# All last tokens formed at the start: a cross-attention kernel whose context is cut into 512-token parts of 528-column rows

## What is computed

```python
x = x + xattn(layernorm(x), ctx_1024, ...)   # 16 heads of 32, 1601 context tokens a batch, stablemax weights
x = x + attn(layernorm(x), ...)              # 8 heads of 64, causal, inside a batch
x = x + ffn(layernorm(x), ...)               # 2 shared experts and the top 2 of 8, hidden 2048
# stablemax: s = where(v >= 0, v + 1, 1 / (1 - v)); s / sum(s)
```

## Time and profile before

| | us |
|---|---|
| median of three runs | 1272.42 (1272.4 to 1272.51) |
| the profiled execution | 1272.52 |
| its span, first to last instruction | 1270.8 |
| TensorE matmuls, busy | 1260.8 |
| VectorE, busy | 649.4 |
| ScalarE, busy | 634.2 |
| GpSimd, busy | 437.4 |

### The profile page before, as it was taken

How to read it: one execution, slowest core, us unless ns; L and a number is a source line. 1 busy time by engine, 2 the same in 40 slices (tenths; PEclk the granted TensorE clock), 3 DMA queues, 4 the chain that set the end, 5 groups by cost and what they waited for, 6 DMA issues and landing times.

```text
span 1270.8 us, 29915 instructions
## 1 busy us (share of the span) xinstructions
PE 1260.8 (99%) x13126; PEld 1097.3 (86%) x13126; DVE 649.4 (51%) x936; ACT 634.2 (50%) x1085; POOL 437.4 (34%) x203
## 2 busy tenths in 40 slices
PE   9999999999999999999999999999999999999998
PEld 8888888888788888888789789798989999999997
DVE  5333453444463363463354454766776555565655
ACT  4445454464545544545444646646544443554443
POOL 1445345544555545545546535200032000100000
PEclk9999999999999999999999999999999999999999
DMA  6131011021011012012012111764556499999990
GB/s 244 50 103 51 18 56 50 23 68 67 19 64 68 18 56 101 19 64 68 18 51 105 51 56 43 284 255 157 179 195 224 148 348 365 340 344 347 357 396 35
DMA packets 32775, 174.89 MB, mean 138 GB/s; under 512 B 5944, under 2 KB 8152, under 8 KB 14464
## 3 DMA queue, kind: packets, MB, share of 16 engines
q1 hardware_dynamic: 30896, 168.16, 36.0%
q0 software_dynamic: 1744, 4.76, 1.2%
HBM read 166.84 MB, written 6.06 MB: 136 GB/s over the span
## 4 chain that ended last, share of the span: by engine, by line
PE 98%; DVE 1%; DMA 0%; ACT 0%; issue 0%; DVEq 0%; SPq 0%
PE bank L740 23%; PE bank L728 22%; PE bank L1079 11%; PE sc L1096 9%; PE sc L756 8%; PE sc L941 7%; PE bank L769 4%; PE sc L960 3%; PE bank L960 3%; PE bank L833 1%; PE bank L796 1%; PE bank L887 1%; PE bank L898 1%; PE sc L898 1%; DMA ctxt<-in_ctx 0%; PE sc L999 0%
## 5 line engine op out<-in xcount | busy, mean ns | idle before, releaser
L587 POOL TENSOR_TENSOR xn<-xn,tt 128x1024 f32<-128x1024 f32 x96 | 230.1, 2397 | 330.9 <-DVE tt L1325 329.7
L1208 ACT ACTIVATE tt<-sc 128x512 f32<-128x512 f32 (+1 forms) x208 | 107.8, 602 | 351.5 <-PE sc L756 351.4
L1423 DVE TENSOR_TENSOR wsl<-ring,wsh 128x2048 fp32r<-128x2048 f32 x72 | 166.8, 2316 | 111.0 <-ACT wsh L1163 107.9
L1312 DVE TENSOR_SCALAR kk<-bank,bkt 128x512 f32<-128x512 f32 (+2 forms) x130 | 80.8, 622 | 213.6 <-PE bank L728 213.2
L728 PE MATMUL bank<-cxh,wkh 128*128 128x512 f32 (+2 forms) x512 | 181.1, 354 | 1.5 <-DVE va L1320 1.0
L728 PE MATMUL bank<-cxl,wkh 128*128 128x512 f32 (+2 forms) x512 | 174.6, 341 | 0.0
L728 PE MATMUL bank<-cxh,wkl 128*128 128x512 f32 (+2 forms) x512 | 174.1, 340 | 0.0
L740 PE MATMUL bank<-wvh,cxh 128*128 128x512 f32 (+1 forms) x416 | 163.5, 393 | 0.0
L740 PE MATMUL bank<-wvl,cxh 128*128 128x512 f32 (+1 forms) x416 | 162.7, 391 | 0.0
L740 PE MATMUL bank<-wvh,cxl 128*128 128x512 f32 (+1 forms) x416 | 162.2, 390 | 0.0
L1163 ACT CAST wsh<-ring 128x2048 fp32r<-128x2048 f32 x72 | 137.4, 1909 | 48.0 <-PE sc L1096 20.9
(11 more groups left out here) (270 smaller groups left out, 2024.2 us busy)
## 6 DMA issues: line engine op xcount, KB each, us to landing
ring<-in_w SPq DMA_DIRECT2D x112, 1024.0 KB, 6.1
ctxt<-in_ctx SPq DMA_DIRECT2D x15, 1024.0 KB, 4.9
ctxt<-in_ctx SPq DMA_DIRECT2D x8, 642.0 KB, 3.9
ctxt<-in_ctx SPq DMA_DIRECT2D x10, 512.0 KB, 3.6
wqt<-in_wo SPq DMA_DIRECT2D x4, 1024.0 KB, 4.8
wqt<-in_aq SPq DMA_DIRECT2D x4, 1024.0 KB, 5.3
wqt<-in_ap_ SPq DMA_DIRECT2D x4, 1024.0 KB, 6.9
yrows<-K SPq DMA_DIRECT2D x1, 2048.0 KB, 9.1
```

The costliest lines, as they stand in the source:

```text
L587: e.tensor_tensor(dacc[0:kn, y, :], dacc[0:kn, y, :], tt[0:kn, w, :], ALU.add).then_inc(s["da_pool"], 1)
L1423: e.tensor_tensor(wsl[m % 3][:], ring[slot(unit_split(m))][:], wsh[m % 3][:].bitcast(F32), ALU.subtract).then_inc(s["wl_dve"], 1)
```

## The change

- The last 65 tokens of all eight batches are one extra load (`tails`), 520 columns in a row of 528. At the start all their keys are formed, as 48 matmuls of 260 columns each for batches 0 to 3 and 4 to 7 (`tail_keys`), and their values in five groups (`tail_values`): four of 128 tokens, each two batches' 64 tokens, and one of the eight very last tokens. Keys and values are stored to memory (`ktail`, `vtail`).
- In each batch SP loads the batch's tail keys back into `ktb` (`load_tail`, slot 1) and its tail values into their slot of `va` (`load_tail_values`, slot 11).
- The rest is 24 parts of 512 tokens; each has four key groups of 512 columns and four value groups. The key groups of a batch's first part move one slot back, to its slots 9 to 12 of the batch before. Slot 10 of a batch has no value group, slot 8 no key group.
- For chunks 99 to 102 the value group stands in the slot of its own number, before it was so for 101 to 103. Chunk 103, a tail, has none.
- The queries are three rounded products of 16 matmuls of 512 columns, with high and low parts of x (`xTh`, `xTl`) and of the weights.
- The start is put in a new order: tail keys, tail values between the turns of x, queries, the keys of part 0 (now 512 tokens), values 0 and 1. Loads of wk, tails, wv, x and wq come in halves.
- Rows of `cxh`, `cxl`, `ctxt` and `kk` have 528 columns, of which a part fills 512. Pads are put between buffers. GpSimd's descriptor scratch goes from its default to 4096 bytes.

```diff
-SPANS = ((0, 512), (512, 512), (1024, 256), (1280, 321))
-WID = 512
+WID = 528
+TAIL = 65
-NPART = len(PARTS)
+NPART = 3 * NB
...
 def key_groups(slot):
+    groups = []
     for i in range(1, NPART):
+        f = first(i - 1) + ((i - 1) % 3 == 2)
+        groups += [(i, slot - f)] * (0 <= slot - f < 4)
+    return groups
...
 def values_in(slot):
-    if slot + 2 < NCH - 3:
-        return slot + 2
-    return slot if NCH - 3 <= slot < NCH else None
+    if slot + 2 < NCH - 5:
+        return None if is_tail(slot + 2) else slot + 2
+    return slot if NCH - 5 <= slot < NCH - 1 else None
...
-    uses = [("k", 0, g) for g in range(4)] + [("v", 0), ("v", 1)]
+    uses = [("vt", j) for j in range(5)] + [("k", 0, g) for g in range(4)] + [("v", 0), ("v", 1)]
...
+        ktb = sb("ktb", [P, 2, 4, TAIL])
+        ceh, cel = sb("ceh", [P, 4, 8], F32R), sb("cel", [P, 4, 8], F32R)
+        sb("pad9", [P, 8])
...
+            for h in range(2):
+                c = slice(2 * h, 2 * h + 2)
+                e.dma_start(wkt[:, c, :], wk[:, c, :]).then_inc(wk_in[h], 16)
+                e.dma_start(tail_raw[:, c, :], tails[:, c, :]).then_inc(tails_in[h], 16)
...
+            def load_tail(b):
+                if b >= 2:
+                    e.wait_ge(s["s_pe"], PER * (b - 1))
+                e.dma_start(ktb[:, b % 2, :, :].rearrange("p g n -> p (g n)"),
+                            ktail[:, 4 * TAIL * b:4 * TAIL * (b + 1)]).then_inc(s["kt_in"], 16)
+            def load_tail_values(b):
+                n = PER * b + PER - 1
+                e.wait_ge(s["p_pe"], n - VR + 1)
+                e.dma_start(va[0:TAIL, n % VR, :], vtail[b]).then_inc(s["vt_in"], 16)
...
+            def tail_values(j):
+                dst, kn = take("vt", j), (8 if j == 4 else P)
+                if j < 2:
+                    e.wait_ge(s["kt_dve"], 8 + 2 * j + 2)
...
             def turn(t, dst):
                 e.wait_ge(s["xn_dve"], t + 1)
+                if t < 2:
+                    e.wait_ge(s["kt_dve"], 16)
+                else:
+                    e.wait_ge(s["xt_dve"], t - 1)
...
+            tail_values(0)
+            tail_values(1)
             for t in range(2):
                 turn(t, bank[2 + t])
+            tail_values(2)
             for t in range(2, 4):
                 turn(t, bank[t])
+            tail_values(3)
+            tail_values(4)
+            e.wait_ge(s["xt_dve"], 4)
             for g in range(4):
+                queries(g)
+            for g in range(4):
+                keys(0, g)
             for n in range(2):
                 values(n)
...
+            for g in range(4):
+                tail_keys(0, g)
+            for h in range(2):
+                e.wait_ge(x_in[h], 16)
                 for t in range(2 * h, 2 * h + 2):
                     stats_of(0, t)
                 for t in range(2 * h, 2 * h + 2):
                     rows(0, t)
+                for g in range(2 * h, 2 * h + 2):
+                    tail_keys(1, g)
...
-    nc = bacc.Bacc("TRN2", target_bir_lowering=False, num_devices=1)
+    nc = bacc.Bacc("TRN2", target_bir_lowering=False, num_devices=1, dynamic_dma_scratch_size=4096)
```

More of the change, by code:

```diff
@@ L45, in first, with is_tail, tokens, place @@
 def first(i):
[L47 to L63, removed]
+    return PER * (i // 3) + 4 * (i % 3)
+def is_tail(n):
+    return n % PER == PER - 1
+def tokens(n):
+    return TAIL if is_tail(n) else P
+def place(n):
+    b, j = divmod(n, PER)
+    return 3 * b + j // 4, j % 4
+def formed(n):
+    return (PER - 1) * (n // PER) + n % PER
 def key_groups(slot):
-    early, late = [], []
+    groups = []
     for i in range(1, NPART):
[L70 to L79, removed]
+        f = first(i - 1) + ((i - 1) % 3 == 2)
+        groups += [(i, slot - f)] * (0 <= slot - f < 4)
+    return groups
 def ending(slot, lag):
@@ L196, in build @@
         xn = sb("xn", [P, 4, D])
+        with ExitStack() as over:
+            xTh = over.enter_context(nc.sbuf_tensor("xTh", [P, 4, D], F32R))
         with ExitStack() as over:
@@ new lines, in tail_values @@
+            def tail_values(j):
+                dst, kn = take("vt", j), (8 if j == 4 else P)
+                col = 260 * (j // 2) + P * (j % 2)
+                if j < 2:
+                    e.wait_ge(s["kt_dve"], 8 + 2 * j + 2)
+                if j == 4:
+                    e.wait_ge(s["tl_dve"], 3)
+                for c in range(4):
+                    if j == 0 and c % 2 == 0:
+                        e.wait_ge(s["wvl_dve"], c // 2 + 1)
+                    for x_, (a, b) in enumerate(three):
+                        m = e.matmul(dst[0:kn, :], (ceh, cel)[a][:, c, :] if j == 4 else
+                                     (cxh, cxl)[a][:, 1, c, col:col + P], (wvh, wvl)[b][:, c, :],
+                                     start=(c == 0 and x_ == 0), stop=(c == 3 and x_ == 2))
+                m.then_inc(s["vt_pe"], 1)
@@ L744, in scores @@
             def scores(n):
-                i, k, kn = chunk(n)
-                u, b, c0 = i % 2, n // PER, 256 * (n - group_of(n)[0])
+                i, k = place(n)
+                b, c0, kn = n // PER, 256 * (n - group_of(n)[0]), tokens(n)
                 if n >= 2:
@@ L755, in scores @@
                         r = slice(32 * h, 32 * h + 32)
-                        m = e.matmul(sc[0:kn, h, c0 + 64 * g:c0 + 64 * g + 64], kk[r, u, g, k * P:k * P + kn],
-                                     qc[r, g, 64 * b:64 * b + 64], start=True, stop=True)
+                        key = ktb[r, b % 2, g, :] if is_tail(n) else kk[r, i % 2, g, k * P:k * P + P]
+                        m = e.matmul(sc[0:kn, h, c0 + 64 * g:c0 + 64 * g + 64], key, qc[r, g, 64 * b:64 * b + 64],
+                                     start=True, stop=True)
                 m.then_inc(s["s_pe"], 1)
             def weighted(n):
-                kn, b = chunk(n)[2], n // PER
+                kn, b = tokens(n), n // PER
                 head, tail = n % PER == 0, n % PER == PER - 1
-                e.wait_ge(s["proj_read"], use["v", n] + 1)
+                if tail:
+                    e.wait_ge(s["vt_in"], 16 * (b + 1))
+                else:
+                    e.wait_ge(s["proj_read"], use["v", n] + 1)
                 e.wait_ge(s["f_dve"], 2 * n + 2)
@@ L1032, in pe @@
                     denominators(b)
-                for i, g in early + late:
+                for i, g in key_groups(n):
                     keys(i, g)
@@ L1201, in act @@
                 for m in group(n):
-                    kn = chunk(m)[2]
+                    kn = tokens(m)
                     if m >= TR:
@@ L1502, in vector @@
             e.tensor_copy(kio[:], iotai[:, P:P + 120].rearrange("p (k e) -> p k e", e=8)).then_inc(s["iota_dve"], 1)
-            values(0)
-            values(1)
+            for g in range(4):
+                keys(0, g)
+            for n in range(2):
+                values(n)
             count = [0]
@@ L1651, in vector @@
                     weights(m, 1)
-                for i, g in late:
-                    keys(i, g)
                 for b, g, m in finished(n)[1]:
```

345 lines of the change are left out of this document (207 added, 138 removed).

## The result

The changed kernel takes 1277.72 us (median of 8 runs, 1274.45 to 1278.83), the kernel before 1272.41 us: a ratio of 1.0037, 95% interval 1.0027 to 1.0046. It is slower by 0.4%, where 1263.3 us and "faster" at 0.91 were forecast. Its times spread over 4.4 us, those of before over 0.3 us, and they lie in groups: 1274.5 (granted clock 0.998 over the run) and 1277 to 1279 us (0.995 to 0.996). The profiled execution is one of the first group: 1274.46 us, span 1272.7 us.

The account below looks back on a forecast made before the run. TensorE was taken as the bound, 98% of the chain at full clock. Its work and joints -16.0, start +0.5, end of the context part +6.3 gave -9.2: 1263.3 us, range 1258.8 to 1267.5, with "faster" at 0.91.

Parts of the forecast that it names:

- the pitch ("I take 0"): Rows of cxh, cxl and kk at 2112 bytes for 2048: claimed to cost TensorE 0.
- Layout: Buffer places and row pitch: nothing moves within 64 bytes, only the pitch changes; 0, at most -30 if faster.
- rival C: The new pitch lengthens TensorE's intervals, 0.09 us for each of 192 groups: +17.3, 1280.6 us, chance 0.07.
- The end of the context part: Hand-over: 3.8 us up to weighted(100), 2.3 before weighted(103), +6.3 together; bounds 2.3 and 8.
- the pairs: Slots 97 and 98 form only keys; the pair lasts 9.2 for a chain of 9.4: 0.2 us.
- A and the joints: TensorE's groups: removed 575.2, added 558.4; joints +0.8; so -16.0. Rival A: hand-over hidden, 1257.0 us, chance 0.13.
- the margin in the chain of the scores' weights: Loop: shortest pair 11.4 us against a chain of 9.3; margin 2.0, so no wait, 0.
- B, more is late: Later loads and copies at the start, or the loop's 11.4 us pair longer than its chain: 1268 us, chance 0.12.
- the page set beside the sum: Skill page's matmul gap, 216 ns for 512 columns: TensorE's part -12 instead of -16.8, 1268 us, no chance of its own.
- The start: First key matmul to scores(0): waits of 1.4 us for 0.9, so +0.5; bounds 0 and +3.

Follow-up runs that it names:

- e9: The changed kernel with useless bf16 products filling TensorE's waits before weighted(100) and weighted(103): 1272.79 us, ratio 1.0003.
- e10: The changed kernel with row pitch 2304 bytes for 2112 and useless bf16 products in the waits before weighted(100) and weighted(103): 1265.97 us, ratio 0.9950.
- a1: The changed kernel again, nothing edited, on the chip of e9 and e10: 1277.09 us (1274.17 to 1278.04).
- m1: Only groups of twelve 512-column fp32r matmuls, computation left out, at several pitches, shifts and starts: 227 ns a product at best, 231.8 at pitch 2112.
- e1: The kernel before with only the row pitch changed, 2112 bytes for 2048, and pads in the expert part: 1276.87 us, ratio 1.0035.
- e5: The changed kernel with row pitch 2304 bytes in place of 2112: 1270.79 us (1267.32 to 1271.89).
- e3: The changed kernel with VectorE's weights_split(0) issued behind the copy of values(100) instead of ahead of it: 1271.04 us.
- e2: The changed kernel with the loop's rows back at 2048 bytes, only the start's tail part keeping 2112: 1270.3 us, ratio 0.9981.
- e6: The changed kernel with row pitch 2304 bytes and weights_split(0) issued behind the copy of values(100): 1264.29 us.
- e11: The changed kernel with pitch 2304, weights_split(0) behind values(100)'s copy, shared_up(0) one slot later, and half of VectorE's normalising one slot later: 1262.98 us, ratio 0.9930.

## Why the prediction was wrong

By its own steps, with the sizes of e9 and e10:

| step | forecast | measured |
|---|---|---|
| the sum with no cost of pitch and no fall of the clock | 1263.3 | 1266.0 (e10) |
| the pitch ("I take 0") | 0 | +6.8 (e9 less e10) |
| the clock behind the waits | not in the sum | +4.3 (a1 less e9), 1.4 to 6.0 by run |
| the changed kernel | 1263.3 | 1277.1 (a1), 1277.7 (first eight runs) |

**Layout is the step that failed.** "No row has such a pitch; I take 0." I weighed the pitch as rival C and gave it 0.07, on an argument that the rows did not carry: fp32 matmuls at pitch 2048 had no extra of 13 ns, "so the extra seems not to come from the pitch" (their "two passes" were themselves only read out of the 216 ns). That spoke of the 13 ns at 2048, which indeed stay at every pitch (227 ns at best in m1), and said nothing about what 2112 would add. The row that did carry it was the one I priced C with, the value group with 65 tokens at 2.81: an interval may grow by 7 ns with the same stream. C's mechanism is what happened, at little more than half its price: 0.05 instead of 0.09 on the 125 groups that follow another, 0.02 on the other 67, 8.2 us for 17.3, and 6.8 in the kernel's time. C's row was no measure of it: the same form is cheaper at the new pitch (2.74 us in e1), so it told only that an interval can change, and why it is dear at 2048 stays open. With neither the pitch's cost nor the clock's the change gains 6.4 us (e10 against its own runs of before, 1272.4); with it and no fall of the clock it takes 1272.8 (e9), level with before. So this step alone takes the time out of the forecast's range, and so does the next: e5, without the pitch's cost but with the clock's, takes 1270.8.

**The end of the context part: right in its waits, short of their price.** Forecast were 3.8 us up to weighted(100) and 2.3 before weighted(103), 6.3 in all with the pairs; measured are 3.1, 2.2 and 0.9 in the scores, 6.2. The ranking of VectorE's work behind ScalarE's cast and GpSimd's sum was as described, and e3 shows the order on VectorE to be the cause. But a wait was priced at its own length. In its last part or behind it the clock is at half for 3.4 or 6.8 us, which put another 1.4 to 6.0 us on the two together, and which of these a run gets differs from run to run.

**A and the joints.** The counts and durations of what is removed and added hold: with the pitch at a multiple of 256 bytes (e10) the kernel takes 1266.0, 2.7 us above the sum. Two rows are dearer by 3.7 together, so something else is 1.0 cheaper than forecast: scores(0) is 0.5 us later than 63.2 (63.72 in e10), and the waits for VectorE's va copy are 4.2 us where before had 1.0. The forecast saw the margin in the chain of the scores' weights, 2.0 us, and not the other ring, the two banks of the projections: with narrower groups gone, TensorE comes for a bank 2.72 us after the last, at the slot where VectorE first normalises a batch (read from the timelines, not tested). "B, more is late" named the loop, but looked for it at the scores. On the page set beside the sum: the same section of the Trainium skill, "TensorE: Matmul & The Clock Gate", "Back-to-back issue gap", calls its N/2.4 + 2.5 the gap of an isolated matmul. The 227 ns here are those of a stream, so they are no measure of that formula.

**The start** cost 0.85 us more than forecast with the new pitch, 0.5 without it, well inside the bound of 3.

Not separated: what in e10's 2.7 us makes up for the 1.0 by which the rows just named exceed it.

## What to carry to other kernels

Before a pitch or a pad is changed on a buffer that TensorE reads, ask where each matmul's moving operand starts against its stationary one: here every difference tried that was not a multiple of 256 bytes cost 2 to 7 ns per 512-column fp32r matmul with 128 stationary columns, and multiples of 256 cost nothing. Price a new wait of TensorE of two microseconds or more together with the half clock that may follow it, and when a kernel's times suddenly spread, look at the granted clock by short windows behind its longest waits. Work of no use in such a wait is a quick test of that, and a cheap remedy while the wait itself is not yet removed.

## What the runs showed of the hardware

- fp32r matmuls of 512 columns, 128 stationary, came at 227 ns with operands a multiple of 256 bytes apart, 229.3 with the moving one 64 or 320 bytes further, and 232 to 234 at the others tried, the same with the other engines idle and busy, and at five common starts (m1).
- Behind the weighted sums' small matmuls the spacing is irregular, 224 to 240 ns, for some ten matmuls before it settles at 227; such a group takes 2.99 us for 2.72, 0.11 of that in its first interval (e10).
- The value group with 65 stationary tokens took 2.81 us with a row pitch of 2048 bytes and 2.74 with 2112 (before, e1).
- TensorE's clock was at 1.2 GHz for 3.4 or 6.8 us, starting between 1.4 us before and 1.5 us behind the end of waits of 2.2 to 3.1 us, at nine of the ten such waits in the profiles (changed kernel, a1, e2, e3, e5, e6); a wait of 1.6 us near the end of every kernel was not followed by it within 4 us; with bf16 matmuls of ones in the same waits the profiles of e9 and e10 have no such stretch, and the mean clock of all their 16 timed runs was 0.999 to 1.0.
- A VectorE cast of 128x128 took 2.27 us beside a GpSimd sum (e11), and 0.23 alone (e10).
